# Layer 1's selection test in two steps, shorter redo, five score tiles, two jobs on GpSimd, and orders dealt anew

## The reference, cut to what matters

```python
# layer 0: full softmax attention, then experts of width 512
x = x + tanh(g_xattn[0]) * L0_xattn(layernorm(x), ctx)
x = x + tanh(g_ffn[0]) * L0_ffn(layernorm(x))
# layer 1: attention over the 32 greatest scores of each row
scores = einsum('bhqd,bhkd->bhqk', q, k) / SCALE
top_scores, top_idx = top_k(scores, 32)
w = softmax(top_scores)
out = einsum('bhqk,bhqkd->bhqd', w, top_v)
# layer 1's second half: self attention plus experts of width 128
expert_out = einsum('bsd,edf->bsef', x, W_experts) + b_experts
moe_out = einsum('bsef,bse->bsf', expert_out, combine)
x = x + tanh(g_ffn[1]) * (attn_out + moe_out)
```

## Time and profile before

| | |
|---|---|
| median of 3 runs | 5476.27 us (5466.68 to 5484.45) |
| profiled execution, its own time | 5464.69 us |
| span of its instructions | 5462.9 us |
| mean granted TensorE clock | 0.875 of full |
| TensorE busy | 4452.0 us, 81% of the span |
| VectorE busy | 4287.1 us, 78% |
| ScalarE busy | 3963.7 us, 73% |
| GpSimd busy | 1154.4 us, 21% |

### The profile page before, as it was taken

How to read it: one execution, slowest core, us unless ns; L and a number is a source line. 1 busy time by engine, 2 the same in 40 slices (tenths; PEclk the granted TensorE clock), 3 DMA queues, 4 the chain that set the end, 5 groups by cost and what they waited for, 6 DMA issues and landing times. The chain is left out here.

```text
span 5462.9 us, 111091 instructions
## 1 busy us (share of the span) xinstructions
PE 4452.0 (81%) x34502; PEld 1713.4 (31%) x34502; DVE 4287.1 (78%) x22093; ACT 3963.7 (73%) x5192; POOL 1154.4 (21%) x2648
## 2 busy tenths in 40 slices
PE   4777678898787989698798989897897888888765
PEld 1324124242332424233242424233242333324211
DVE  4457987978888887988888787888878888876771
ACT  1346767878586887778688787876887687877673
POOL 2121112222122222212122222211222122121110
PEclk7778889999798999899899999988898898988776
DMA  4232222322122232222223222322222122220100
GB/s 121 70 79 53 58 68 59 81 65 74 49 66 72 59 80 65 67 57 67 71 60 79 63 76 59 78 68 54 75 62 71 51 75 61 52 61 23 35 25 19
DMA packets 472183, 344.99 MB, mean 63 GB/s; under 512 B 155897, under 2 KB 454140, under 8 KB 471550
## 3 DMA queue, kind: packets, MB, share of 16 engines
q1 hardware_dynamic: 471550, 337.54, 24.4%
HBM read 230.12 MB, written 107.13 MB: 62 GB/s over the span
## 5 line engine op out<-in xcount | busy, mean ns | idle before, releaser
L943 DVE MAX8 cand<-s 128x8 f32<-128x67 f32 (+1 forms) x12288 | 1986.2, 222 | 174.0 <-DVEq L1083 122.0
L914 ACT ACTIVATE prob<-wide 128x1024 f32<-128x1024 f32 (+1 forms) x1792 | 1735.0, 1031 | 233.0 <-PE wide L631 102.7
L1029 DVE TENSOR_REDUCE part<-score 128x1 f32<-128x1024 f32 (+1 forms) x1024 | 1003.5, 980 | 303.5 <-PE score L586 261.3
L680 PE MATMUL att<-prob,v 128*9 128x256 f32 (+1 forms) x14336 | 1193.8, 412 | 21.1 <-ACT prob L914 19.7
L895 ACT ACTIVATE s<-wide 128x1024 f32<-128x1024 f32 (+1 forms) x1024 | 821.8, 841 | 390.2 <-DVEq L1083 232.5
L631 PE MATMUL wide<-q,k_att 64*128 64x256 bf16 (+1 forms) x6656 | 700.0, 288 | 260.1 <-ACT s L895 120.8
L904 ACT ACTIVATE below<-wide 128x1024 bf16<-128x1024 f32 (+1 forms) x832 | 819.3, 1027 | 74.6 <-PE wide L631 71.7
L1272 POOL TENSOR_SCALAR flag<-cand,ends 128x24 bf16<-128x24 f32 x512 | 178.9, 349 | 2460.0 <-DVE ends L968 1959.9
L656 PE MATMUL wide<-below,minus_ident 128*128 128x512 bf16 (+1 forms) x1664 | 527.7, 405 | 120.5 <-ACT below L904 104.2
L586 PE MATMUL score<-k_scan,q 64*128 64x512 bf16 (+1 forms) x2048 | 451.5, 365 | 183.2 <-DVE part L1029 159.4
L601 PE MATMUL wide<-k_scan,q 64*128 64x512 bf16 (+1 forms) x2048 | 430.0, 368 | 144.9 <-ACT s L895 79.7
(11 more groups left out here) (161 smaller groups left out, 5124.8 us busy)
## 6 DMA issues: line engine op xcount, KB each, us to landing
k_stack<-split_b SPq DMA_DIRECT2D x576, 128.0 KB, 2.4
k_att<-k_stack SPq DMA_DIRECT2D x768, 96.0 KB, 2.3
k_scan<-k_stack SPq DMA_DIRECT2D x512, 96.0 KB, 2.3
ctxT<-in_ctx_dram SPq DMA_DIRECT2D x32, 800.5 KB, 4.5
k_scan<-k_stack SPq DMA_DIRECT2D x512, 48.0 KB, 1.8
q<-q_stack SPq DMA_DIRECT2D x256, 96.0 KB
q_stack<-split_b SPq DMA_DIRECT2D x192, 64.0 KB, 2.1
self_stack<-split_b SPq DMA_DIRECT2D x192, 64.0 KB, 2.1
```

Of the source, the lines that this page charges most:

```text
L680: r = tensor.matmul(att[32 * j:32 * j + HD + 1, 0:S], v[0:kc, c, j0 * HG + j, :], m.prob[n % 3][0:kc, j * S:(j + 1) * S], start=(c == 0), ...
L914: scalar.activation(pr[0:kc, :], ps[0:kc, :], ACT.Exp, scale=SCALE).then_inc(sem["wide_done"], 1)
L943: i = vector.max(cand[:, :, c], s[:, KCUT[c]:KCUT[c + 1]])
L1029: vector.tensor_reduce(m.part[:, QT * hh + qt, c:c + 1], score[:, 0:wd], AX.X, ALU.max).then_inc(sem["score_max"], 1)
```

## The change

There are five parts.

1. **Test in two steps.** `check` is divided: `count` does the reduction of the flags, and `check`, a step or so later in VectorE's list, loads the number and branches. Between them stands another step, which of a round's 16 pairs is in 8 an `n0_max` or a `z_max` (one of them with a short `ln_aggr` ahead of it), in 5 a `rank` (once with an `o_norm`), in 2 a single short step, and in 1 nothing.
2. **Six passes in a redo.** The first MAX8 over the whole tile is left out, since the merge has the 8 greatest already; a tile takes three MATCH_REPLACE8 and three MAX8.
3. **Five tiles held.** `s` has five tiles (`HELD`); the copy of a tile waits for the check of the pair in which the tile five before it is.
4. **GpSimd sums layer 1's experts and scales the normed rows.** `z_add` becomes a product and an addition for each expert (15 instructions), and `ln_scale` moves unchanged. Each has a semaphore that tells VectorE and TensorE.
5. **The tables** `ORDER` and `LAG` are new throughout: the same steps for each engine but for those moved, in another sequence.

```diff
+HELD = 5
-    ln_stats=("normed", 1), ln_aggr=("normed", 2), ln_scale=("normed", 1), n0_max=("score_max", 1),
-    z_max=("score_max", 1), n0_all=("n0_ready", 1), check=("checked", 2), least=("least_done", 5),
+    ln_stats=("normed", 1), ln_aggr=("normed", 2), n0_max=("score_max", 1),
+    z_max=("score_max", 1), n0_all=("n0_ready", 1), count=("counted", 1), check=("checked", 1), least=("least_done", 5),
...
-        "rows_out.0": 9, "k_att.0": 36, "rows_in.0": 9, "k_scan.0": 30, "k_scan.1": 57, "rows_out.1": 16,
+        "k_att.1": 65, "k_att.0": 36, "k_scan.0": 30, "k_scan.1": 58, "rows_out.0": 9, "rows_in.0": 9, "q_in.1": 14,
...
-                        if tile >= 4:
-                            q.wait_ge(sem["checked"], after("check", (tile - 4) // 8, (tile - 4) % 8 // QT))
-                        scalar.activation(m.s[tile % 4][:, a0:a0 + wd], ps[:, 0:wd],
+                        if tile >= HELD:
+                            q.wait_ge(sem["checked"], after("check", (tile - HELD) // 8, (tile - HELD) % 8 // QT))
+                        scalar.activation(m.s[tile % HELD][:, a0:a0 + wd], ps[:, 0:wd],
...
+                    elif name == "count":
+                        q.wait_ge(sem["small_full"], after("flag", *key))
+                        vector.tensor_reduce(m.many[:, :], small[0:1, 0:QT * (KC + 1)], AX.X,
+                                             ALU.max).then_inc(sem["counted"], 1)
+
                     elif name == "check":
                         g, pair = key
-                        done, tile = before(name, *key), scan_tile(g, QT * pair)
-                        q.wait_ge(sem["small_full"], after("flag", *key))
-                        if done:
-                            q.wait_ge(sem["checked"], done)
-                        vector.tensor_reduce(m.many[:, :], small[0:1, 0:QT * (KC + 1)], AX.X, ALU.max).then_inc(sem["checked"], 1)
-                        q.wait_ge(sem["checked"], done + 1)
+                        tile = scan_tile(g, QT * pair)
+                        q.wait_ge(sem["counted"], after("count", *key))
                         vector.reg_load(many_reg, m.many[0:1, 0:1])
                         with vector.If(vector.snap(many_reg, min_val=0, max_val=P) > 0):
...
-                                for i in range(TOPK // 8):
-                                    if i:
-                                        vector.match_replace(s[:, :], best[i - 1], s[:, :], NEG).then_inc(redo, 1)
...
+                                for i in range(1, TOPK // 8):
+                                    vector.match_replace(s[:, :], best[i - 1], s[:, :], NEG).then_inc(redo, 1)
...
                                     vector.max(best[i], s[:, :]).then_inc(redo, 1)
...
                         vector.nop(nofuse=True).then_inc(sem["checked"], 1)
...
-                    elif name == "z_add":
...
             @block.gpsimd
...
+                    elif name == "ln_scale":
+                        kind, b = key
+                        q.wait_ge(sem["pow_done"], after("ln_pow", *key))
...
+                        for t in range(QT):
+                            i = gpsimd.tensor_scalar(m.xn[:, t, :], m.x[b % 5][:, t, :], m.mv[:, t, 0:1],
+                                                     m.rstd[:, t:t + 1], ALU.subtract, ALU.mult)
+                        i.then_inc(sem["scaled"], 1)
+
+                    elif name == "z_add":
...
+                        gpsimd.tensor_scalar(r.acc[:, t, :], y[:, 0:D], r.one[:, t, 0:1], None,
+                                             ALU.mult).then_inc(sem["z_added"], 1)
+                        for e in range(1, E):
+                            part = m.z_part[e % 2]
+                            if e > 2:
+                                q.wait_ge(sem["z_added"], done + 2 * e - 3)
+                            gpsimd.tensor_scalar(part[:, :], y[:, e * D:(e + 1) * D], r.one[:, t, e:e + 1], None,
+                                                 ALU.mult).then_inc(sem["z_added"], 1)
+                            q.wait_ge(sem["z_added"], done + 2 * e)
+                            gpsimd.tensor_tensor(r.acc[:, t, :], r.acc[:, t, :], part[:, :],
+                                                 ALU.add).then_inc(sem["z_added"], 1)
```

More of the change, by code:

```diff
@@ L89 @@
[L89 to L93, removed]
@@ L136 @@
     pool="""
[L137 to L140 removed]
+        mark*2 shift.0 mark shift.1 mark*2 ln_pow.z ln_scale.z mark split.z_qk*2 mark z_add mark z_add mark*2 ln_pow.w
@@ L167 @@
+        "route_exp.z": 5, "att_copy.0": 9, "o_copy.0": 3, "row_minus.2": 20, "w_k_out.0": 4, "ln_copy.w": 1,
+        "w_v_out.0": 4, "w_q_out": 1, "ln_copy.v": 3, "exp_z": 40, "route_exp.v": 3, "v_gelu": 24, "att_copy.2": 20,
         "ln_copy.u": 3, "u_q_out": 3, "w_k_out.1": 8},
     dve={
-        "n0_all": 9, "rank": 478, "n0_max": 128, "check": 61, "least": 16, "o_norm.1": 17, "x_add.1": 5,
-        "ln_stats.z": 5, "ln_aggr.z": 5, "ln_scale.z": 5, "route_best.z": 5, "ln_stats.w": 1, "route_pick.z": 5,
@@ L171 @@
-        "z_add": 10, "ln_aggr.w": 1, "o_norm.0": 9, "x_add.0": 3, "z_max": 40, "ln_scale.w": 1, "ln_stats.v": 3,
-        "ln_aggr.v": 3, "ln_scale.v": 3, "route_best.v": 3, "route_pick.v": 3, "v_add": 24, "x_add.v": 3,
-        "o_norm.2": 20, "ln_stats.u": 3, "ln_aggr.u": 3, "ln_scale.u": 3, "x_add.z": 5},
+        "o_norm.0": 10, "n0_all": 9, "rank": 482, "count": 62, "n0_max": 128, "check": 62, "least": 16,
+        "o_norm.1": 17, "x_add.1": 5, "ln_stats.z": 5, "ln_aggr.z": 5, "route_best.z": 5, "route_pick.z": 5,
@@ L250, in streams @@
     of("mark", "mark", [(n,) for n in range(QT * HG * NG)])
-    for name in ("flag", "check"):
+    for name in ("flag", "count", "check"):
         of(name, name, [(g, hh) for g in groups for hh in range(HG)])
@@ L344, in build @@
     copies = T.number("act", "att", ("att_copy",))
-    norms = T.number("dve", "norm", ("ln_scale",))
-    assert norms == [("ln_scale", k) for n, k in T.steps["dve"] if n == "ln_stats"]
+    norms = T.number("pool", "norm", ("ln_scale",))
+    stats_of = [k for n, k in T.steps["dve"] if n == "ln_stats"]
+    assert norms == [("ln_scale", k) for k in stats_of]
     T.number("pool", "split", ("split",))
@@ L417, in build @@
         m.xnT["u"] = m.xnT["v"]
+        m.z_part = [sb(f"z_part{n}", [P, D]) for n in range(2)]
         wide = [psum(f"wide{n}", 2 * BANK) for n in range(2)]
@@ L489, in small_drain @@
                 return "z_v_out", key
-            return "check", key
+            return "count", key
         def stored(name, key):
@@ L564, in _ @@
                         ps = claim(name, *key)
-                        q.wait_ge(sem["normed"], after("ln_scale", kind, b))
+                        q.wait_ge(sem["scaled"], after("ln_scale", kind, b))
                         turned(ps, lambda t: m.xn[:, t, :])
```

207 lines of the change are left out of this document (99 added, 108 removed), and 2 rows, old and new, of the table sp.

## The result

The changed kernel takes 5482.26 us (median of 20 runs, 5461.07 to 5506.08), the kernel before 5469.94 in the same comparison (20 runs, 5451.90 to 5484.45): ratio 1.0031, 95% interval [1.0017, 1.0045]. The forecast was 5307 us; it is 3.3% off and has the wrong sign. The profiled execution took 5491.77 us, with a span of 5489.7.

A forecast was written before the change was run, and what follows sets the result against it. It took VectorE (88% of a clean round) as full as TensorE (89%) but seldom waited for. Relief worth 120 us, redo 29 and fifth tile 20 made 169 us off 5464.7: 5296, on the median's scale 5307; range 5150 to 5435.

The forecast's parts named there:

- I take 8 us: Full rounds: of VectorE's relief of 18.6 us a round, 8 us become time, 120 us over 15 rounds.
- Rival B: Full rounds: TensorE and ScalarE, passing two buffers, are the bound; only 2 us a round come, 5397 us; chance 0.22.
- raises the clock a little: Full rounds: less idle time also raises the granted clock; given beside the 8 us, with no size of its own.
- I book no change for the ramp and the tail: Program's two ends: the new orders keep about the same depth in rounds, so no time is booked.
- Two steps: VectorE's checks: another step covers the sequencer's pauses; 131 of 192.6 us go, 62 us stay.
- Rival C: VectorE's checks: the load waits for an empty engine, so the divided test brings nothing; 5359 us; chance 0.08.
- `z_add` on GpSimd: Layer 1's expert sums: 7.5 us each on GpSimd (6.9 to 8.8), relieving VectorE of 111 us.
- Rival D: Marks behind `z_add`: GpSimd's sums hold them up, delaying VectorE and TensorE; slower, 5547 us; chance 0.08.
- Shorter redo, 29 us: Redos: 8 redos × 2 tiles × 1.829 us = 29.3 us, all of which counts as everything waits.
- Five tiles, 20 us: Redos: TensorE goes on sooner after the copy, 8 × 2.5 = 20 us; ends 0 and 60.
- Port, 3 us: VectorE's small SBUF additions: slowed while GpSimd works more, charged at 0.2 us a round, 3 us.
- Signs set out beforehand: Changed kernel's trace: VectorE busy 4117 us, signal idle under 80, redo pauses 20 to 23, clean rounds 293, flag waits unchanged.

The follow-up runs named there:

- f_less_vector: The kernel before, but VectorE reads only the first quarter of the score columns in `n0_max`; 5415.64 us, ratio 0.9914.
- e_old_orders: The changed kernel with the lists of the kernel before, only `count`, `z_add` and `ln_scale` set where they must be; 5431.81 us, ratio 0.9940.
- e_gpsimd: The kernel before with only `z_add` and `ln_scale` moved to GpSimd, `count` directly ahead of each `check`; 5463.42 us, ratio 0.9998.
- e_six_five: The kernel before with six passes in a redo and five tiles held, orders as before; 5420.96 us, ratio 0.9924.

## Why the prediction was wrong

- **"I take 8 us", the worth of the relief in a round: failed, and most of the error.** The relief itself came (pauses gone, busy 4143.6). It passes on some 7% of net, not 43%: 2.5 of 37.1 us in f_less_vector, and clean rounds of equal net length, 283.3, before and after (282.6 with two steps alone, 281.4 in e_old_orders). 15 rounds at 8 us were 120 of the 169 us. Rival B had the amount (2 us a round), with a wrong owner: the pair of engines, where less work on ScalarE left net at 283.0. I had read TensorE at 89% of a round and took the rest as room for VectorE's relief; what fills that room is not shown. I also wrote that less idle time "raises the clock a little". In the changed kernel the time at 1.2 GHz went up, 36.2 to 45.1 us in a clean round.
- **"I book no change for the ramp and the tail": failed.** New lists cost 43 us in the start and about 50 in all (5431.81 against 5482.26). "The depth in rounds ... is about the same" was true and beside the point: at the start it counts how many `n0` stand ahead of a step.
- **Two steps:** the mechanism was right and the size too small. I kept 62 us for pairs with little cover; 2.2 + 8.9 = 11.1 us are left. Rival C is out. The Trainium skill, Advanced Engine Details and Errata, Sequencer and Instruction Queues, which the sum left aside, says that other engine instructions can be read and queued while a control instruction is carried out. The trace agrees: 192.6 to 11.1 us.
- **`z_add` on GpSimd:** 8 × 0.602 + 7 × 0.455 + 18.7 / 32 = 8.6 us, not 7.5, inside the ends of 6.9 to 8.8. The product with a scalar was mis-sized, 0.602 for 0.43. `ln_scale` takes 0.793 us for 0.43. GpSimd's total is 1505 for 1440. With the old lists neither is seen to hold anything up: e_gpsimd is 0.9998. Two of D's signs did come in the changed kernel, rounds over 305 us and longer waits for the flag product; but 123.3 us in e_old_orders against 204.0 puts the longer waits on the new lists, and the clean rounds' waits end behind TensorE's work, not GpSimd's. Rival D is out as it was told, though 8.6 us is above the 7.5 that it was built on.
- **Shorter redo, 29 us: borne out.** 48 MAX8, and eight pauses shorter by 25.3 us in e_six_five.
- **Five tiles, 20 us: not seen.** e_six_five gained 41 us, with an interval of about 14 us to either side. If 29 of them are the passes, as expected, 12 are left, less than the interval; pauses and a sixth tile show nothing.
- **Port, 3 us:** too small to be seen in these runs.
- **Signs set out beforehand:** VectorE 4144 (4117), pauses under 80, 48 MAX8 and pauses of 18.1 to 23.1 us in a redo (20 to 23) came, nearly. The waits for the flag product did not stay near what they were (204.0 us for 111.1). Clean rounds of 305.8 us lie outside 287 to 299, the mark by which the prediction was to be wrong.

The account of the profiled executions: start +33.9, eleven rounds −8.0, rest +0.8, together 26.7 us (5486.4 − 5459.7, at the last L1149 and its counterpart). The medians differ by 12.

## What to carry to other kernels

Share the busy time of each engine out by stage, and then try the owner: give each engine less to do, one at a time, and see which relief shortens which stage. An engine at 89% with short handovers between can be the bound. Where TensorE paces, read the granted clock before you remove its work: relief can cost more than it gives (3.2% here), and a few full-array products ahead of a weak stage can give more than they cost (1% at `z_moe`), but not ahead of every one (at `s_z` the same filling lost 0.4%). And when written orders are dealt anew together with a mechanism, run the mechanism in the old orders as well: here that told a gain of 0.6% from a loss of 0.9%.

## What the runs showed of the hardware

- The granted clock fell to 0.51 in `z_moe` (f32 products, half of them of one row), with TensorE busy for 17.10 of 17.10 us and for all of the 10.20 us ahead of them, and 32 bf16 products of 128 columns a round in that stage kept it at 1.00. Removing the one-row products did not.
- Taking 18.8 us of products out of a round raised its half-clock time from 36 to 97 us, and the kernel lost 3.2%.
- GpSimd: 128x128 f32 with one scalar operand 602 ns, with two 793 ns, sum of two tiles 455 ns; VectorE's are 282, 459 and, multiplying in as well, 352 ns.
- A load and branch on VectorE's sequencer that stood 0.76 us behind a reduction cost VectorE 2.2 us in all, and 8.9 us behind the reduction, once another step stood between.
